# Attention with Strassen-like weight splits: seven splits of each next weight matrix placed at other units of the step, GpSimd's four sums of it spread out, and the load of the matrix after it later in SyncE's queue

## The reference, cut to what matters

```python
q, k, v = proj(x, Wq), proj(x, Wk), proj(x, Wv)          # x: (8, 512, 1024), W: (1024, 1024), 16 heads of 64
q = q * minimum(cond, 4.0)
scores = einsum('bhqd,bhkd->bhqk', q, k) / sqrt(64)       # causal mask, softmax
out = einsum('bhqk,bhkd->bhqd', softmax(scores), v)
y = einsum('bsd,ed->bse', out, Wo)
x = x + einsum('bsi,oi->bso', int8_like(y), ternary(weight)) + bias
```

## Time and profile before

| what | value |
| --- | --- |
| median of 3 runs | 2069.6 us (2066.71 to 2071.45) |
| the profiled execution, its time | 2065.57 us |
| its span (first to last instruction) | 2063.6 us |
| granted TensorE clock, mean | 0.986 |
| PE busy | 1949.7 us, 94% |
| DVE, ACT, POOL busy | 66%, 50%, 44% |

### The profile page before, as it was taken

How to read it: one execution, slowest core, us unless ns; L and a number is a source line. 1 busy time by engine, 2 the same in 40 slices (tenths; PEclk the granted TensorE clock), 3 DMA queues, 4 the chain that set the end, 5 groups by cost and what they waited for, 6 DMA issues and landing times.

```text
span 2063.6 us, 40315 instructions
## 1 busy us (share of the span) xinstructions
PE 1949.7 (94%) x12378; PEld 1695.6 (82%) x12378; DVE 1365.8 (66%) x3331; ACT 1025.5 (50%) x2495; POOL 908.2 (44%) x984
## 2 busy tenths in 40 slices
PE   8999889899998999998999989999986999999998
PEld 6788667899988999988999988999975777777775
DVE  6545664577788777778777788777775645455454
ACT  4443333477776777777777677677773000000000
POOL 1333343244455444455444455444452544444441
PEclk9999999999999999999999999999998999999999
DMA  6899998777767777776777776777752432333332
GB/s 214 326 373 353 350 339 332 280 280 257 254 239 287 259 258 258 263 273 247 267 254 278 259 254 241 261 275 248 262 192 81 133 122 92 112 102 103 110 98 75
DMA packets 165696, 477.83 MB, mean 232 GB/s; under 512 B 12768, under 2 KB 84448, under 8 KB 135776
## 3 DMA queue, kind: packets, MB, share of 16 engines
q1 hardware_dynamic: 165072, 476.11, 65.8%
q10 hardware_dynamic: 528, 0.52, 0.1%
HBM read 331.88 MB, written 111.15 MB: 215 GB/s over the span
## 4 chain that ended last, share of the span: by engine, by line
PE 69%; DVE 13%; DMA 6%; issue 6%; ACT 4%; POOL 2%; SPq 1%; DVEq 0%; ACTq 0%; POOLq 0%
PE proj_ps L209 19%; PE s_ps L571 9%; PE proj_ps L571 8%; PE t_ps L985 6%; PE o_ps L642 5%; PE t_ps L335 5%; PE o_ps L373 5%; PE o_ps L985 4%; DMA parts<-x_scratch 3%; DVE pt_all L359 2%; PE s_ps L295 2%; PE s_ps L296 2%; DVE q_st L272 2%; DMA xv_raw<-xT 2%; DVE prob L307 2%
## 5 line engine op out<-in xcount | busy, mean ns | idle before, releaser
L209 PE MATMUL proj_ps<-parts 128*128 128x256 f32 x5376 | 768.6, 291 | 8.0 <-DMA parts<-x_scratch 7.9
L209 PEld LDWEIGHTS proj_ps<-parts 128*128 128x128 f32 x5376 | 677.4, 192 | 19.8 <-DVE k_sum L244 7.1
L325 POOL TENSOR_TENSOR prob<-prob,row_inv 128x128 f32<-128x128 f32 (+3 forms) x512 | 371.9, 727 | 623.2 <-DVE row_inv L319 623.2
L313 ACT ACTIVATE prob<-prob,row_min 128x128 f32<-128x128 f32 (+3 forms) x512 | 287.6, 562 | 202.8 <-DVE row_min L307 198.1
L359 DVE TENSOR_TENSOR pt_all<-t_ps,pt_all 128x128 fp32r<-128x128 f32 (+3 forms) x512 | 249.1, 487 | 110.4 <-ACT pt_all L352 110.3
L307 DVE CUSTOM_DVE_ANT_0 prob<-s_ps,mask 128x128 f32<-128x128 f32 (+3 forms) x512 | 247.1, 483 | 32.5 <-PE s_ps L296 7.0
L335 PE MATMUL t_ps<-ident,prob 128*128 128x128 f32 x1280 | 229.9, 278 | 35.0 <-DVE pt_all L359 30.5
L627 ACT ACTIVATE yt_q<-t_ps 128x1024 bf16<-128x1024 bf16 x32 | 32.7, 1023 | 426.7 <-PE t_ps L620 426.7
L352 ACT ACTIVATE pt_all<-t_ps 128x128 fp32r<-128x128 f32 (+3 forms) x512 | 216.4, 423 | 5.8 <-PE t_ps L335 4.1
L335 PEld LDWEIGHTS t_ps<-ident,prob 128*128 128x128 f32 x1280 | 150.7, 141 | 64.2 <-issue 37.4
L295 PE MATMUL s_ps<-k_sw,q_st 128*128 128x128 f32 (+3 forms) x512 | 170.1, 332 | 30.3 <-DVE row_min L307 25.4
(11 more groups left out here) (124 smaller groups left out, 2814.8 us busy)
## 6 DMA issues: line engine op xcount, KB each, us to landing
parts<-x_scratch SPq DMA_DIRECT2D x224, 1024.0 KB, 7.7
x_scratch<-xv SPq DMA_DIRECT2D x112, 512.0 KB, 5.9
k_sw<-k_st SPq DMA_DIRECT2D x128, 256.0 KB, 3.7
xv_raw<-xT SPq DMA_DIRECT2D x17, 1024.0 KB, 8.8
v_scratch<-v_tmp SPq DMA_DIRECT2D x64, 256.0 KB, 5.1
v_raw<-v_scratch SPq DMA_DIRECT2D x32, 512.0 KB, 3.8
oT_scratch<-o_sum SPq DMA_DIRECT2D x64, 256.0 KB, 3.6
o_raw<-oT_scratch SPq DMA_DIRECT2D x32, 512.0 KB, 4.6
```

The lines of the kernel that those rows point to most:

```text
L209: mm = pe.matmul(qk_bank(w, m), wc[w][:, c, wp, k, :], xq[:, c, :, xp, k, :], start=(fresh and k == 0 and i == 0), stop=(k == CH - 1 and i ...
L313: act.activation(prob[u % QT], prob[u % QT], ACT.Exp, bias=row_min[:, u % 4:u % 4 + 1], scale=-1.0, accum_out=row_sum[:, u % 4:u % 4 + 1]) ...
L325: pool.tensor_tensor(prob[u % QT], prob[u % QT], row_inv[:, u % 4:u % 4 + 1].broadcast_to([P, w]), ALU.mult).then_inc(norm_done, 1)
```

## The change

It does five things in the steps that make the splits. The seven splits of Wk stand in slots 1, 2, 4, 6, 7, 8, 9 before, and in 4, 8, 10, 12, 12, 13, 13 after. Those of Wq for groups 1 to 3 go from the same seven slots to 2, 4, 8, 9, 10, 12, 13; for group 0 they stay. GpSimd's sums S1 and S3 stand at the start of the step before and after `N(1)` and `N(2)` now; S2 and S4 stand after `N(0)` before and after `N(3)` and `N(5)` now. `load_w` moves in SyncE's queue from behind x for product 1 to behind x for product 4. No work is added or removed.

```diff
+        K_SPLITS = {4: (0,), 8: (1,), 10: (2,), 12: (3, 4), 13: (5, 6)}
+        Q_SPLITS = {2: (0,), 4: (1,), 8: (2,), 9: (3,), 10: (4,), 12: (5,), 13: (6,)}
+        Q_SPLITS_FIRST = {1: (0,), 2: (1,), 4: (2,), 6: (3,), 7: (4,), 8: (5,), 9: (6,)}
...
-            if qk_for is not None:
-                w_first_sums(pool, 2 * qk_for)
-            if late_for is not None:
-                w_first_sums(pool, 2 * late_for + 1)
...
             N(0)
-            if qk_for is not None:
-                w_last_sums(pool, 2 * qk_for)
-            if late_for is not None:
-                w_last_sums(pool, 2 * late_for + 1)
             N(1)
+            WS(S1)
             N(2)
+            WS(S3)
             N(3)
+            WS(S2)
             SV(old, 3)
             N(4)
             N(5)
+            WS(S4)
...
                 load_xq(sp, nxt[0], nxt[2], M_P1)
                 load_xq(sp, nxt[0], nxt[2], M_P2)
-            if qk_for is not None:
-                load_w(sp, 2 * qk_for + 1)
-            if late_for is not None and late_for + 1 < NG:
-                load_w(sp, 2 * late_for + 2)
             if nxt:
                 load_xq(sp, nxt[0], nxt[2], M_P6)
...
+            if qk_for is not None:
+                load_w(sp, 2 * qk_for + 1)
+            if late_for is not None and late_for + 1 < NG:
+                load_w(sp, 2 * late_for + 2)
             if nxt:
                 load_xq(sp, nxt[0], nxt[2], M_P3)
```

More of the change, by code:

```diff
@@ L440, in load_w, with w_sum @@
             sp.dma_start(w_raw, (wk, wq)[n % 2][n // 2, :, :, :]).then_inc(qk_in, 16)
[L442 to L455, removed]
+        def w_sum(pool, n, c):
+            a11, a12, a21, a22 = w_quad(0, 0), w_quad(0, 1), w_quad(1, 0), w_quad(1, 1)
+            if c == S1:
+                pool.wait_ge(qk_in, (n + 1) * 16)
+                pool.tensor_tensor(w_extra, a21, a22, ALU.add).then_inc(qk_sum_done, 1)
+            elif c == S3:
+                pool.wait_ge(qk_in, (n + 1) * 16)
+                pool.tensor_tensor(a21, a11, a21, ALU.subtract).then_inc(qk_sum_done, 1)
+            elif c == S2:
+                pool.wait_ge(qk_lo_done, 7 * n + 1)
+                pool.wait_ge(qk_sum_done, 4 * n + 2)
+                pool.tensor_tensor(a11, w_extra, a11, ALU.subtract).then_inc(qk_sum_done, 1)
+            else:
+                pool.wait_ge(qk_lo_done, 7 * n + 2)
+                pool.wait_ge(qk_sum_done, 4 * n + 3)
+                pool.tensor_tensor(a12, a12, a11, ALU.subtract).then_inc(qk_sum_done, 1)
@@ new lines, in adaln_ffn_kernel, with split_parts @@
+        K_SPLITS = {4: (0,), 8: (1,), 10: (2,), 12: (3, 4), 13: (5, 6)}
+        Q_SPLITS = {2: (0,), 4: (1,), 8: (2,), 9: (3,), 10: (4,), 12: (5,), 13: (6,)}
+        Q_SPLITS_FIRST = {1: (0,), 2: (1,), 4: (2,), 6: (3,), 7: (4,), 8: (5,), 9: (6,)}
+        def split_parts(eng, unit, qk_for, late_for, low):
+            if qk_for is not None:
+                for m in K_SPLITS.get(unit, ()):
+                    split_w(eng, 2 * qk_for, m, low)
+            if late_for is not None:
+                for m in (Q_SPLITS if late_for else Q_SPLITS_FIRST).get(unit, ()):
+                    split_w(eng, 2 * late_for + 1, m, low)
@@ L1266, in v_pool @@
                 if n == PAIRS - 1:
-                    w_first_sums(pool, 0)
-                    w_last_sums(pool, 0)
+                    for c in (S1, S3, S2, S4):
+                        w_sum(pool, 0, c)
                 v_ur(pool, n)
@@ L1461, in act_step @@
             E(3)
-            W(3)
+            W(6)
             H(1)
@@ L1479, in act_step @@
             E(7)
+            W(10)
             if last and now:
@@ L1495, in act_step @@
             E(10)
+            W(13)
             H(8)
@@ L1613, in dve_step @@
             M(10)
+            W(12)
             L(7)
@@ L1639, in SV, with WS @@
                     split_v(pool, step[0], h)
-            if qk_for is not None:
-                w_first_sums(pool, 2 * qk_for)
-            if late_for is not None:
-                w_first_sums(pool, 2 * late_for + 1)
+            def WS(c):
+                if qk_for is not None:
+                    w_sum(pool, 2 * qk_for, c)
+                if late_for is not None:
+                    w_sum(pool, 2 * late_for + 1, c)
             N(13)
```

40 lines of the change are left out of this document (18 added, 22 removed).

## The result

The changed kernel takes 2076.9 us in the median (2072.2 to 2078.2), the kernel before 2069.0 on the same chip. The ratio is 1.0037, with a 95% interval of 1.0026 to 1.0049: slower by 7.9 us, where +8.4 was forecast. The profiled execution took 2078.21 us, its span is 2076.1 us: 12.5 us over the span before. So the two profiles stand further apart than the medians. In what follows I compare spans.

The account below looks back on a forecast made before the run. PE, at 94% of the span, was taken as the bound, with special steps waiting for DVE. -31.9 + 22.8 (B and C) + 12.9 (D) + 4.6 (E) = +8.4 us on 2069.6 gave 2078.0 us; range 2072 to 2084.

Parts of the forecast that it names:

- D: Steps 8, 16 and 24: Wq lands late, PE stands still 4.3 us before `T(15)`, three times: 12.9 us.
- E: Steps 9 and 17: x for product 5, behind the matrix, is late; 4.6 us in all, nothing in step 1.
- The part that is removed: Six special steps (three K, three Q): PE's extra waiting from splits and sums goes, 31.9 us won.
- B: Slots 6 to 10: sum S2 and DVE-GpSimd port conflicts delay `N(4)`; 1.25 us per K step, 2.1 per Q step.
- C: Splits in slots 12 and 13 make `L(8)` late; 2.6 us per K step, 1.65 per Q step.
- Cover: Rival: D and E hold, but DVE's splits find pauses; B and C 11 to 14 us, kernel 2067.5; chance 0.13.

Follow-up runs that it names:

- the last kernel above: Changed kernel with Wk's splits ending in slot 12, Wq's load ahead of K's swap, next Wk last, sums S1, S3, S2 one unit earlier: 2046.4 us.
- e_fill: The filled kernel: changed kernel, in steps 8, 16, 24 the half product before `S(2)` moved behind it, eighteen overwritten matmuls ahead of it: 2076.1 us, ratio 1.0030.
- e_k_old: Changed kernel with the next Wk's load last in the queue and the K step's splits and sums at their old places: 2072.7 us, ratio 1.0024.

## Why the prediction was right, and where only its sum was

The time and the sign came out as forecast, by the path forecast: D and E cost more than the new places win. But four of its terms were off, and their errors cancelled; that the sum came within a microsecond of the measured difference is luck. The six special steps and the three behind them are 42.3 us over nine times the 35.51 us of step 9 of the kernel before, where they were 32.1; with step 1, which is 2.9 us longer, that is +13.1 us in this pair of profiles.

- **The part that is removed**, taken at 31.9 us, is shown in its mechanism and not in its full size. The 1.67 us before `S(0)` is 0.42 now, in step 7. But the last kernel above still has 12.4 us of excess in its six special steps, so no run shows all of it won; what follows for B and C is what is left when it is taken whole. One split stays in slot 8 of a K step, where the prediction had none between 5 and 9.
- **Terms B and C**, forecast at 22.8 us, cost 9.5 (what is left of the 42.3 after the parts below). *Cover*, at 11 to 14, came nearest. The step that failed is the one that sent each delay to PE whole. On C: two splits in a row took 1.34 and 1.41 us and not 1.56 (the split of 0.78 us that I called alone began while an `N` was running, from 617.35 to 617.75; really alone it takes 0.69), and DVE's pauses took up nearly all of the rest, since `L(8)` delays PE by 0.22 us and not 1.2. The last slot of a K step is 0.6 to 0.8 us longer. On B: one wait of 0.49 us for `N(4)` in step 7, where slots 9 and 10 are 0.9 us longer together and 1.25 was given; in steps 15 and 23 the wait for x below comes first, and none is left. In Q steps a part of B is not absent but hidden behind D, as the filled kernel showed (1.22 us for `N`). What did come as forecast is the carry into the next step: 0.7 us in its slots 0 and 1, under the 1.1 given.
- **Term D** had the mechanism, the place and the wait: 4.3 forecast, 3.66, 4.62 and 5.48 measured. The step that failed is that a wait costs its length. Slots 4 and 5 of the three Q steps hold 21.8 us over their normal 4.1 each, not 12.9, of which the idle time is 13.8; the rest is PE at 1.2 GHz behind it. The range for the landing (down to 10.2, not above 10.8) was also on the wrong side: 10.3, 11.3, 12.4.
- **Term E** had the mechanism and missed half of the places: 7.1 us in steps 9 and 17 (with 0.7 each for the carry of C taken off) and 2.9 in step 1, against 4.6. I had looked at x for product 5 alone, and x for product 6 is late too; step 17 pays for the clock as well. "In step 1: nothing" was wrong, by its argument that the bytes ahead are the same: what counts is when PE asks, and the waits of 1.60 and 1.48 us stand there where one of 0.51 stood.
- **Not forecast:** waits for x for product 6 of 1.3 and 1.4 us in slot 7 of steps 15 and 23, some 3 us with that slot's whole lengthening. Also 0.8 us in step 25, ahead of which no matrix is loaded: it stays with the next Wk last (36.96 against 37.02 us), so it isn't E, and PE waits there 0.84 us for the swap of K and 0.47 us for x. A K step without its stalls comes sooner to the swap of K's block 1: it is issued 14.4 us into step 23 (at 1215.4), before it was 17.5 us (at 1206.6). It now meets x for product 6 in flight, which lands 14.3 us after its issue, not 11.7. With the K part undone it lands in 11.5 and there is no wait. The kernel before shows the same meeting and wait in step 26.

In all: B and C 13 us too dear, D 9 and E 5 too cheap, some 4 us forgotten. With B and C right and the rest as forecast I would have said 2064.7, on the wrong side. The forecast's own range, 2072 to 2084, holds the time only because the errors cancelled.

What the rest of the change did is now clear too. The new places of the splits and sums are good, by 7 to 10 us for Wk alone. The place of the load eats it. With Wk's splits ending in slot 12 and Wq ahead of the swap, and the next Wk last in the queue, the same idea is 19 to 21 us faster than the kernel before.

## What to carry to other kernels

When the DMA engines are full for a stretch (their share stood at 0.9 to 1.1 at 330 to 450 GB/s from 643 to 653 us of the changed kernel), every transfer in it has a price, and the question is which one is asked for last: put the transfer that is used six steps later behind all others, and make what gates an urgent one end a slot sooner. When a wait is taken away, write down what is late behind it; here the load's wait passed in turn to the swap of K, to x and to `N`. And when waits on PE of several microseconds are priced, look at the clock behind them: here the stillness cost more than half as much again (21.8 us lost for 13.8 us of waiting).

## What the hardware showed unexpectedly

The granted clock fell to 0.50 after waits of 3.66 us (before `T(15)`), 2.71 us (x in the kernel with later splits of Wq) and 3.58 us (before `S(0)` with both loads back), and stayed at 1.00 after one of 1.40 us in the filled kernel and of 1.67 us in the earlier trace rows. Behind the first, twelve matmuls took 2.91 and then 2.27 us against 1.68. This looks like a limit on the length of a wait, and it isn't one: the clock fell after 1.66 us in step 23 of e_k_old and after 1.99 us of waiting for x in step 17 of e_fill, and it stayed at 1.00 after 2.21 us in step 9 and 3.56 us in step 24 of e_fill. Between 1.6 and 3.6 us these runs show both; every wait over 3.6 us in steps 2 to 25 of them was followed by the low clock.

The port that DVE and GpSimd share cost less than I had reckoned. GpSimd's rows of K step 7, S2 and the split of V beside DVE's q_st pair:

```profile
616.84 1.30 POOL L454 TENSOR_TENSOR w_raw<-w_raw 128x512 f32<-128x512 f32 x1
618.09 0.62 POOL L428 TENSOR_TENSOR v_st<-v_raw,one 128x256 fp32r<-128x256 f32 x1
618.78 1.07 POOL L431 TENSOR_TENSOR v_st<-v_raw,v_st 128x256 fp32r<-128x256 f32 x1
```

Only the last of the three is held up (1.07 against 0.73 in the earlier trace rows). In step 7 a split beside an `N` took 1.31 us against 0.69 alone (the one at 649.65), but the q_st pair was held up by 0.4 us in all. The Trainium skill, "SBUF — State Buffer", section "Who interferes with whom", has the port pair that the two engines share as an exclusive lock, and a DVE instruction with two inputs in SBUF contend with a GpSimd instruction that reads SBUF. The single pairs agree with it. Why the q_st pair lost 0.4 us here and 1.25 us in the earlier trace rows was not tried.
